# Seven quadrant products in place of eight for the second square layer of the last three tiles

## The reference, cut to what matters

```python
h = silu((x @ w1.T) * w1_s) * ((x @ w2.T) * w2_s)      # 256 -> 1024
h = gelu((h @ h1.T) * h1_s)                            # 1024 -> 1024, the first square layer
h = gelu((h @ h2.T) * h2_s)                            # 1024 -> 1024, the second square layer
out = (h @ w3.T) * w3_s                                # 1024 -> 256
# x = x + 0.5 * block(layernorm(x)); x = x + attn(layernorm(x)); x = x + 0.5 * block(layernorm(x))
```

## Time and profile before

| what | value |
|---|---|
| time, median of 3 runs | 1422.49 us (1422.36 to 1422.56) |
| span of the profiled execution, first to last instruction | 1420.9 us |
| TensorE busy | 1415.5 us, 100% of the span |
| VectorE busy | 986.1 us, 69% |
| ScalarE busy | 478.9 us, 34% |
| granted TensorE clock, mean over the core | 1.000 |
| transfers | 80.28 MB, mean 56 GB/s |

### The profile page before, as it was taken

How to read it: one execution, slowest core, us unless ns; L and a number is a source line. 1 busy time by engine, 2 the same in 40 slices (tenths; PEclk the granted TensorE clock), 3 DMA queues, 4 the chain that set the end, 5 groups by cost and what they waited for, 6 DMA issues and landing times.

```text
span 1420.9 us, 17300 instructions
## 1 busy us (share of the span) xinstructions
PE 1415.5 (100%) x6923; PEld 1164.5 (82%) x6923; DVE 986.1 (69%) x1742; ACT 478.9 (34%) x724; POOL 48.8 (3%) x43
## 2 busy tenths in 40 slices
PE   9999999999999999999999999999999999999999
PEld 4888888888878888788787888878878788888887
DVE  7877778675878888758888577784777755354433
ACT  5524342523425124232232332422424223141321
POOL 0000000000000000010000100001000010000000
PEclk9999999999999999999999999999999999999999
DMA  9001000012023111131210312112120112010000
GB/s 365 23 5 40 16 30 30 19 42 67 35 76 145 49 58 60 42 104 60 75 60 12 134 45 74 43 33 100 60 74 15 60 41 74 1 45 0 30 1 16
DMA packets 54434, 80.28 MB, mean 56 GB/s; under 512 B 2768, under 2 KB 46160, under 8 KB 53072
## 3 DMA queue, kind: packets, MB, share of 16 engines
q1 hardware_dynamic: 54352, 79.15, 16.4%
HBM read 57.12 MB, written 22.02 MB: 56 GB/s over the span
## 4 chain that ended last, share of the span: by engine, by line
PE 97%; issue 1%; DMA 1%; DVE 0%; SPq 0%
PE ps L1362 80%; PE ps L1451 8%; PE ps L1502 3%; PE ps L1555 2%; PE ps L1338 1%; PE ps L1434 1%; DMA raws<-in_weights 1%; PE ps L1436 1%; PE ps L1496 1%; PE ps L1497 1%; PE ps L1464 1%; PE ps L1545 0%; PE ps L1479 0%; DVE hid_a_lo L1251 0%; SPq L320 0%
## 5 line engine op out<-in xcount | busy, mean ns | idle before, releaser
L511 ACT ACTIVATE act_o<-ps,scales 128x512 f32<-128x512 f32 x384 | 264.5, 689 | 858.8 <-PE ps L1362 856.8
L1362 PE MATMUL ps<-hid_b_hi,h 128*128 128x512 f32 x1024 | 401.4, 392 | 0.0
L1362 PE MATMUL ps<-hid_b_lo,h 128*128 128x512 f32 x1024 | 398.6, 389 | 0.0
L1362 PE MATMUL ps<-hid_a_hi,h 128*128 128x512 f32 x984 | 386.9, 393 | 0.0
L1362 PE MATMUL ps<-hid_a_lo,h 128*128 128x512 f32 x984 | 383.0, 389 | 0.0
L1362 PEld LDWEIGHTS ps<-hid_b_hi,h 128*128 128x128 f32 x1024 | 192.2, 188 | 41.2 <-issue 1.2
L1362 PEld LDWEIGHTS ps<-hid_b_lo,h 128*128 128x128 f32 x1024 | 192.2, 188 | 40.7 <-issue 1.2
L1362 PEld LDWEIGHTS ps<-hid_a_hi,h 128*128 128x128 f32 x984 | 184.7, 188 | 40.5 <-issue 2.2
L1362 PEld LDWEIGHTS ps<-hid_a_lo,h 128*128 128x128 f32 x984 | 184.7, 188 | 40.2 <-issue 2.2
L1362 PE MATMUL ps<-hid_b_hi,w 128*128 128x512 f32 x480 | 187.2, 390 | 0.0
L1362 PE MATMUL ps<-hid_b_lo,w 128*128 128x512 f32 x480 | 186.8, 389 | 0.0
(11 more groups left out here) (275 smaller groups left out, 1277.6 us busy)
## 6 DMA issues: line engine op xcount, KB each, us to landing
ks<-k_d SPq DMA_DIRECT2D x32, 512.0 KB, 3.8
raws<-in_weights SPq DMA_DIRECT2D x9, 1024.0 KB, 13.7
xin<-in_x SPq DMA_DIRECT2D x8, 512.0 KB, 3.8
x_d<-xin SPq DMA_DIRECT2D x8, 512.0 KB, 2.8
z_d<-xin SPq DMA_DIRECT2D x8, 512.0 KB, 2.8
zb<-z_d SPq DMA_DIRECT2D x8, 512.0 KB, 4.9
wb<-x_d SPq DMA_DIRECT2D x8, 512.0 KB, 4.2
x_d<-wb SPq DMA_DIRECT2D x8, 512.0 KB, 3.5
```

Of the source, the lines that this page charges most:

```text
L511: A(act_o[:, k % ACT_SLOTS], bank(source), func, scale=scale).then_inc(s_act, 1)
L1362: last = MM(o, weight[:, k, cols].bitcast(dt), part[:, k].bitcast(dt), start=(k == 0 and i == 0), stop=(k == n - 1 and i == len(act_) - 1))
```

## The change

In tiles 13, 14 and 15 the second square layer is made of 2 by 2 quadrants: the 8 input blocks by parity (even, odd), the 512 tokens by halves (`NEAR`, `FAR`), the 8 output blocks by halves. Plainly this takes eight quadrant products; the new code takes seven (the Winograd form of Strassen's scheme) and pays with sums on both sides:

- Sums of the weights (`sums_of_weights`): in tile 13, VectorE makes four sums of quadrants of `h2`, 128 x 2048 each, in two halves, into the space that the spectral work has left, and ORs their words to see whether low bits are set (`join_bits`, `fold_bits`, a reduction, a matmul of one column, `second_flag`). ScalarE issues transfers (`place_sum`) that bring three sums into `hid_b`'s space, and the fourth over a quadrant of `h2`.
- Sums of the activations: `split` of steps 8 to 15 is replaced by `operands_high` on ScalarE and `even_block` and `odd_block` on VectorE. The operands, `alone`, `back` and `front`, are 256 tokens wide. `back` and `front` start at multiples of 512 bytes (`LEAD = 0`). `front` lies over `w1` and `w2`, which ScalarE reloads at the end of tiles 13 and 14; `layer_one` waits for that (`s_rw`).
- The products (`seven_products`): twice seven products of 16 matmuls, 256 wide, in place of 8 steps of 16 matmuls 512 wide. Between them ScalarE copies two results out of PSUM and VectorE adds two (`first_sum`, `second_sum`); `quadrant` and `quadrant_low` take the place of the gelu and the split.
- The program of TensorE has a second branch: after the first square layer of tile 13 the two bodies join (a jump over the float32 body), TensorE waits for `flag_2`, loads it and branches.
- `layer_three` takes the blocks in another order for the near tokens.

The diff, cut to its core:

```diff
+SEVEN_FROM = 13
+HALF = TOK // 2
+NEAR, FAR = slice(0, HALF), slice(HALF, TOK)
+FRONT_CHUNKS = 2
+LEAD = 0
...
+        front, _ = zone(FRONT - LEAD, ("front", [P, 2, 4, 2, HALF], F32R))
...
+        AT = Z0 + (LINE - LEAD) % LINE
+        back, BITS = zone(AT, ("back", [P, 4, 4, 2, HALF], F32R))
...
+        raw_1, raw_2, raw_4, raw_s3, _ = zone(Z0, *((n, [P, 4, TOK]) for n in ("raw_1", "raw_2", "raw_4", "raw_s3")))
...
                 else:
                     load_residual(T)
+                if T == SEVEN_FROM - 2:
+                    for c in range(FRONT_CHUNKS):
+                        sp.dma_start(w_d[:, chunk(c)], a["weights"][:, chunk(c)]).then_inc(s_front, 16)
...
+            def place_sum(n):
+
+                act.wait_ge(s_spare, 2 * n + 2)
...
+                    issue_sum(n, A21, raw_s3[:, :])
+
+            def operands_high(T, k):
+
+                q, slot = (k - KH) // 2, act_o[:, k % ACT_SLOTS]
+                act.wait_ge(s_act, at_u(T, k))
+                if k % 2 == 0:
+                    A(alone(q, 0), slot[:, FAR], ACT.Copy).then_inc(s_hi_a, 1)
+                else:
+                    staging_read(act, T, q)
+                    A(back[:, q, B22:B21 + 1, 0], slot.rearrange("p (h t) -> p h t", h=2), ACT.Copy).then_inc(s_hi_b, 1)
+                    act.wait_ge(s_split, at_split(T, k - 1))
+                    A(back[:, q, T1:T3 + 1, 0], back_f[:, q, T1:T3 + 1, 1], ACT.Copy).then_inc(s_hi_t, 1)
+                    act.wait_ge(s_t4, at_pair(T, q))
+                    A(front[:, :, q, 0], front_f[:, :, q, 1], ACT.Copy).then_inc(s_hi_u, 1)
+
+            def copy_first_product(T, g):
+                act.wait_ge(s_p1, at_block_pair(T, g))
+                act.wait_ge(s_act, at_u(T, 2 * KH + 4 * g - 1))
+                A(bank(3), bank(0), ACT.Copy).then_inc(s_p1c, 1)
+
+            def copy_fifth_product(T, g):
+                act.wait_ge(s_p5, at_block_pair(T, g))
+                A(fifth, bank(1).rearrange("p (m t) -> p m t", m=2), ACT.Copy).then_inc(s_p5c, 1)
+
...
+            def quadrant(T, k):
+
+                g, c = divmod(k - 2 * KH, 4)
+                if c == 0:
+                    copy_first_product(T, g)
+                    copy_fifth_product(T, g)
+                first, tokens = 2 * g + (0, 4, 0, 4)[c], (FAR, NEAR, NEAR, FAR)[c]
+                act.wait_ge(s_u, at_u(T, k))
+                if c == 1:
+                    act.wait_ge(s_sum2, at_block_pair(T, g))
...
+                for i in range(2):
+                    last = A(slot[:, i], bank(c)[:, i * HALF:(i + 1) * HALF], ACT.Gelu,
+                             scale=scales[:, 3, first + i:first + i + 1])
+                last.then_inc(s_act, 1)
+                act.wait_ge(s_act, at_u(T, k))
+                A(hid_a_hi[:, first:first + 2, tokens], slot, ACT.Copy).then_inc(s_chi, 1)
+                if g and T + 1 < ALL:
+                    if c == 0:
+                        issue(flat_of(w2), w_d[:, chunk(1)], s_rw)
+                    if c == 3:
+                        issue(flat_of(w1), w_d[:, chunk(0)], s_rw)
 
             def gated_high(T, m):
                 act.wait_ge(s_gate, at_gate(T, m))
...
+            def even_block(T, k):
+
+                q, slot = (k - KH) // 2, act_o[:, k % ACT_SLOTS]
+                dve.wait_ge(s_act, at_u(T, k))
+                staging_read(dve, T, q)
+                V.tensor_tensor(back_f[:, q, T1, 1], slot[:, NEAR], slot[:, FAR], ALU.subtract).then_inc(s_t1, 1)
+                dve.wait_ge(s_hi_a, at_pair(T, q))
+                V.tensor_tensor(alone(q, 1), slot[:, FAR], alone(q, 0).bitcast(F32),
+                                ALU.subtract).then_inc(s_lo_a, 1)
+
...
+            def odd_block(T, k):
+
+                q, n = (k - KH) // 2, at_pair(T, (k - KH) // 2)
+                even, slot = act_o[:, (k - 1) % ACT_SLOTS], act_o[:, k % ACT_SLOTS]
+                dve.wait_ge(s_act, at_u(T, k))
+                V.tensor_tensor(back_f[:, q, T3, 1], slot[:, NEAR], even[:, NEAR], ALU.subtract).then_inc(s_split, 1)
+                dve.wait_ge(s_t1, n)
+                V.tensor_tensor(front_f[:, T2, q, 1], slot[:, NEAR], back_f[:, q, T1, 1], ALU.subtract).then_inc(s_t2, 1)
+                dve.wait_ge(s_t2, n)
+                V.tensor_tensor(front_f[:, T4, q, 1], slot[:, FAR], front_f[:, T2, q, 1], ALU.subtract).then_inc(s_t4, 1)
+                dve.wait_ge(s_hi_t, n)
+                V.tensor_tensor(back[:, q, T1:T3 + 1, 1], back_f[:, q, T1:T3 + 1, 1],
+                                back[:, q, T1:T3 + 1, 0].bitcast(F32), ALU.subtract).then_inc(s_lo_t, 1)
+                dve.wait_ge(s_hi_u, n)
+                V.tensor_tensor(front[:, :, q, 1], front_f[:, :, q, 1],
+                                front[:, :, q, 0].bitcast(F32), ALU.subtract).then_inc(s_lo_u, 1)
+                dve.wait_ge(s_hi_b, n)
+                V.tensor_tensor(back[:, q, B22:B21 + 1, 1], slot.rearrange("p (h t) -> p h t", h=2),
+                                back[:, q, B22:B21 + 1, 0].bitcast(F32), ALU.subtract).then_inc(s_split, 1)
+
+            def both_of(i):
+                return bank(i).rearrange("p (m t) -> p m t", m=2)
+
...
+            def first_sum(T, g):
+                dve.wait_ge(s_p6, at_block_pair(T, g))
+                if g:
+                    dve.wait_ge(s_act, at_u(T, 2 * KH + 2))
+                dve.wait_ge(s_p5c, at_block_pair(T, g))
+                V.tensor_tensor(both_of(2), both_of(3), fifth, ALU.add).then_inc(s_sum1, 1)
+
+            def second_sum(T, g):
+                dve.wait_ge(s_u, at_u(T, 2 * KH + 4 * g + 1))
+                V.tensor_tensor(both_of(1), both_of(3), fifth, ALU.add).then_inc(s_sum2, 1)
+
...
+                def sums(first, n=1):
+                    for step in range(first, first + n):
...
+                        if step:
+                            dve.wait_ge(s_spare, step)
+                        part = slice(step % 2 * 2, step % 2 * 2 + 2)
+                        out, a_, b_, op = ((raw_1, A21, A22, ALU.add), (raw_2, raw_1, A11, ALU.subtract),
+                                           (raw_4, A12, raw_2, ALU.subtract), (raw_s3, A11, A21, ALU.subtract))[step // 2]
+                        V.tensor_tensor(out[:, part], a_[:, part], b_[:, part], op).then_inc(s_spare, 1)
...
+                def join_bits(first, n=1):
+                    words = lambda i: (raw_1, raw_2, raw_4, raw_s3)[i // 2][:, i % 2 * 2:i % 2 * 2 + 2].bitcast(I32)
+                    both = bits[:, :].rearrange("p (k n) -> p k n", k=2)
+                    for i in range(first, first + n):
+                        dve.wait_ge(s_spare, 7 + i)
+                        V.tensor_tensor(both, words(0) if i == 1 else both, words(i), ALU.bitwise_or).then_inc(s_spare, 1)
...
+                if k < 5:
+                    sums((0, 2, 4, 5, 7)[k], (2, 2, 1, 2, 1)[k])
+                if 5 <= k < 11:
+                    join_bits((1, 3, 4, 5, 6, 7)[k - 5], 2 if k == 5 else 1)
...
+                    dve.wait_ge(s_spare, 18)
+                    V.tensor_reduce(top, bits[:, 0:256], AX_X, ALU.max).then_inc(s_top, 1)
+
+            def second_flag():
+                dve.wait_ge(s_topsum, 1)
+                V.tensor_copy(flag_2[0:1, :], ps[0:1, 4, 0:1]).then_inc(s_spare, 1)
+                dve.wait_ge(s_spare, 19)
+                V.tensor_tensor(flag_2[0:1, :], flag_2[0:1, :], flag[0:1, :], ALU.add).then_inc(s_flag_2, 1)
+
...
                     pe.wait_ge(s_zhi, T)
                     pe.wait_ge(s_zlo, T)
+                    if seven(T):
+                        pe.wait_ge(s_rw, 32 * (T - SEVEN_FROM))
                 elif m == 1:
...
+            def square_product(o, weight, operand, begin, dt, ready=None):
+
+                for q in range(4):
+                    if ready:
+                        ready(q)
+                    for part in range(2):
+                        for i in range(2):
+                            last = MM(bank(o)[:, i * HALF:(i + 1) * HALF], weight(q, i).bitcast(dt),
+                                      operand(q, part).bitcast(dt), start=begin and q == i == part == 0,
+                                      stop=q == 3 and part == 1, skip_group_check=True)
+                return last
+
...
+            def seven_products(T, g, dt):
...
+                between(T, k)
+                pe.wait_ge(s_act, at_u(T, KH + 4) if g == 0 else at_u(T, 2 * KH))
+                square_product(0, even(0), alone, True, dt, since(s_lo_a)).then_inc(s_p1, 1)
+                pe.wait_ge(s_act, at_u(T, KH + 5) if g == 0 else at_u(T, 2 * KH + 1))
+                if T == SEVEN_FROM and g == 0:
+                    pe.wait_ge(s_sum_ld[0], 16)
+                square_product(1, summed(0), of(back, T1), True, dt, since(s_lo_t)).then_inc(s_p5, 1)
+                pe.wait_ge(s_p1c, n)
+                if T == SEVEN_FROM and g == 0:
+                    pe.wait_ge(s_sum_ld[1], 32)
```

(31 more changed lines are left out.)

220 lines of the change are left out of this document (181 added, 39 removed).

## The result

Median 1428.7 us (1427.29 to 1429.86, 4 runs) against 1422.53 (1422.36 to 1422.66, 4 runs): ratio 1.004 [1.0028, 1.0053], 0.4% slower. The profiled execution took 1427.29 us, its trace spans 1425.5 us, 4.6 more than before, at a granted clock of 0.999. The forecast was 1427.8.

The account below looks back on a forecast made before the run. TensorE's stream was taken as the bound, busy for 1415.5 of 1420.9 us. Terms -7.8 + 9.8 + 1.3 + 2.0 = +5.3 us, with 1420.9 + 1.6, gave 1427.8 us; range 1423.3 to 1435.0.

Parts of the forecast that it names:

- The gain: Second square layer, tiles 13 to 15: 224 matmuls of 256 replace 128 of 512, -7.8 us (-10.6 to -6.2).
- the choice of 118.0 ns: Price taken for each 256-wide quadrant matmul, from tile 15's third layer, between 113.8 and 120.4 ns.
- The end of 120.4: Dearest price of a 256-wide matmul with both operands at multiples of 512 bytes: layer 27.0 us, gain 6.2 in all.
- two passes: Plain float32 matmuls on TensorE were said to have two passes, 214.4 ns each for 512 columns and 108.0 for 256.
- VectorE in layer one: Tile 13: eight sums and four ORs between the gates hold up TensorE until step 8's end, +9.8 us (9.0 to 10.8).
- one sign wrong: Expected in the profile of tile 13's first layer: TensorE waiting for `gz` and `hid_a_lo`.
- a sign of being wrong: The prediction is wrong if 256-wide matmuls are above 121 ns or tile 13's first layer is under 22 us.
- The rival of a faster kernel: VectorE's 1024-wide operations take about 0.6 us, so sums hardly hold up TensorE: -7.1 us, 1415.4; chance 0.09.
- The bits: After step 14 of tile 13, TensorE's matmul waits for VectorE's reduction of the low bits: +1.3 us (0.5 to 2.5).
- The jump: Behind step 15 of tile 13, TensorE jumps over the float32 body, loads the flag and branches: +2.0 us (0 to 5.0).
- Other covers: Helper copies, additions, half gelus, the `w1` reload and moved waits in tiles 13 to 15 hide behind TensorE: no cost.
- the thin cover: Third quadrant product needs ScalarE's copy of the first, ready at 3.5 us, wanted at 3.8; failing costs 0.3 us a tile.

Follow-up runs that it names:

- lead64: The changed kernel with its two operand buffers started 64 bytes before a multiple of 512 bytes: 1425.54 us, ratio 1.0016 to the kernel before.
- moved_sums: The changed kernel with `LEAD = 64`, eight of twelve VectorE operations moved out of tile 13's layer one, flag's operations moved, second branch nested: 1413.85 us, ratio 0.9935.

## Why the prediction was right

**Mechanism.** TensorE's stream was the bound, the products' gain was real, and VectorE's sums took more than that back, as the forecast has it. Its sum was +5.3, the trace has +4.6.

**The gain, -7.8 (-10.6 to -6.2): too large, -6.4.** The step that was off is the choice of 118.0 ns. The end of 120.4, pass plus 12.4 ns, was the right one: the 256-wide matmuls are 120.0 ns apart, and 113.4 with the operand 64 bytes earlier. (The "two passes" of plain float32 there are those of one row; the 16 float32 matmuls of `project` leave the 32 rows. The 214.4 and 108.0 ns are not touched by that.) The 118.0 of the kernel before's last third layer is a price of its own, with the same operand at the same place: its 64 matmuls are evenly 117 to 119 ns apart, and so are those of tile 13's third layer here (7.54 us). Why, stays open.

The Trainium skill (TensorE: Matmul & The Clock Gate, Wait — 56ns, not 53.3ns?) gives 109.2 ns for 256 columns, an estimate by its rule of N / 2.4 plus 2.5 ns. The trace does not agree: 120.0 and 113.4 ns at the two places of the operand. The gain of 3.2 us a tile that went with it was 2.15 here and 3.4 with the operand 64 bytes earlier, since the 512-wide ones are slower than that rule as well (226.8 against 215.8 ns).

**VectorE in layer one, +9.8 (9.0 to 10.8): +9.65.** 1.14 us from one addition's start to the next, 1.26 where the next needs its result, no gap: as counted. VectorE's stretch from the first gate to the last `hid_a_lo` took 24.28 us (1178.62 to 1202.90), 0.5 less than forecast, and the lower clock in step 8, which the forecast does not have, made up 0.4: the nearness to 0.15 us is in part luck. It also put one sign wrong: TensorE was to wait for `hid_a_lo`, and no such wait is there, because step 8 ran too slowly to meet it. Layer one itself took 22.26 us (1175.97 to 1198.23), not 24 to 25, and just above the 22 that was named as a sign of being wrong. Without these operations layer one goes back to 226.9 ns a matmul. The rival of a faster kernel needed operations under 0.7 us; they took 1.22.

**The bits, +1.3 (0.5 to 2.5): +1.2, of which the wait that was forecast is 0.74.** VectorE's backlog behind step 8 was worked off faster than I counted: by step 13 it waited 0.15 us for that step's gelu. The bits' own matmul and the slower start of step 15, 0.4 us together, were not in the term.

**The jump, +2.0 (0 to 5): 0.6 to 0.8.** Two parts of the term were too long: the jump took 3.27 us where the row of before has 3.86, and it began 0.1 us after the bits' matmul, where I had put 0.8 for issuing step 15. It ran behind 16 queued matmuls of 3.85 us. It is a price of a far jump all the same: the Trainium skill (Runtime: NRT & Kernel Launch, Instruction fetch mechanics) has a taken branch out of the fetched window wait for a transfer of its code; the trace agrees, with 3.27 and 3.89 us for the two jumps and 87 to 88 ns for the branches that fall through.

Of the idle time that the profile was to show, 1 to 2 us ahead of the bits' matmul and 1 to 3 ahead of the quadrants, there were 0.74 and 0.36.

**Other covers, nothing:** no wait in tiles 14 and 15; the thin cover of the products within a tile held.

**Not in the sum: the end.** I took the timed runs to lie 1.6 us above the span as before. They lie 1.8 above it, and most executions of the change end with the late store, which adds some 2 us to its median. The jump 1.3 us too dear and a gain 1.4 us too large cancelled, and the late store, which the forecast did not have, lifted 1427.3 to 1427.8 to the median of 1428.7. That the number came within 0.9 us is in part luck; that the kernel is slower, and through VectorE's sums, is not.

## What to carry to other kernels

An engine's free time in a stage counts only where its work can lie: 16 us were free in the next layer and 7 at the end of the tile before (6.97 idle ahead of `z_low` in the trace after), 3.2 where the sums were put. With the operands 64 bytes ahead in both, moving eight of the twelve operations there, and the jump out of the way, turned 0.16% slower (`lead64`) into 0.65% faster. Look at where operands start: here the moving operand at a multiple of 512 bytes cost 6.6 ns a 256-wide matmul, in layer three of the kernel before as in the quadrants. Before a difference of 2 us is explained by the main path, look at what follows the last matmul, code transfers among it.

## What I had not expected of the hardware

- Float32r matmuls of 256 columns start 113.4 ns apart, and 120.0 ns with the moving operand (activations or `w3`) at a multiple of 512 bytes, the stationary one being at such multiples throughout. `lead64` has both in one layer. One or two of the sixteen third layers of a trace have 118 ns, unexplained.
- TensorE's granted clock was at the 1.2 GHz level for eight matmuls of step 8, behind 6.2 us of waits in layer one, the longest of 2.4; in `moved_sums`, with 0.2 us of waits, it did not fall.
- A 16 KB fetch of code that began 2.17 to 2.35 us after the last matmul's start made the last 128 KB store, through at 2.56 us otherwise, land 1.65 to 2.05 us later; one begun at 2.42 us or later cost nothing. Without the fetch the store was through at 2.56 us in both traces.
- A jump over a float32 body (3.27 us) costs 0.6 to 0.8 us when a step of 16 matmuls is queued ahead of it.
